# A new order of the routing stage in a fused attention and mixture-of-experts kernel

## The reference

```
xn   = layernorm(x)
out  = x + attention(xn) + shared(xn) + experts(xn)
attention: 16 heads of 128 in 4 groups that share k and v, causal softmax, dense 2048 -> 512
shared(xn) = relu(xn @ Ws1.T)**2 @ Ws2.T                 # 512 -> 512 -> 512
routing:   s = sigmoid(xn @ Wr.T + br)                   # 32 experts, 8 groups of 4
           keep the 4 groups with the largest sum of their two best; then the 6 best experts
           gate = 2.5 * s / sum of the six chosen s
experts:   sum over the chosen e of gate[e] * relu(xn @ W1[e].T)**2 @ W2[e].T
```

## Time and profile before

| | |
|---|---|
| median of 3 runs | 1601.65 us (1601.16 to 1601.92) |
| the profiled execution | 1600.37 us, of which the span of the instructions is 1598.6 us |
| PE busy in the span | 1551.1 us (97%) |
| DVE, ACT, POOL busy | 71%, 53%, 19% |
| chain that ended last | PE 94%, DVE 4%, ACT 1%, issue 1% |
| PE busy by 40th of the span (40 us each), tenths | 6897899899999999999999999999999999999998 |

### The profile page before, as it was taken

The page is one execution under the profiler, slowest core; times in us unless marked ns, Lnnn a source line. Parts: engine busy times, 40 slices in busy tenths (PEclk is TensorE's granted clock), DMA queues, the critical chain, the costliest instruction groups (busy, mean ns, idle before and its releaser), DMA issues.

```text
span 1598.6 us, 31303 instructions
## 1 busy us (share of the span) xinstructions
PE 1551.1 (97%) x8780; PEld 1331.9 (83%) x8781; DVE 1137.6 (71%) x2324; ACT 844.3 (53%) x1756; POOL 296.9 (19%) x542
## 2 busy tenths in 40 slices
PE   6897899999999999999999999999999999999998
PEld 5776789889889878888888888888888888888886
DVE  5586766665665638958967876876885895895886
ACT  3546466766666645535544544544553563553553
POOL 0000544444344401001011011011011111100101
PEclk9899899999999999999999999999999999999999
DMA  7492477777777631112011011422110211211101
GB/s 265 158 371 104 168 229 238 235 242 220 243 243 240 212 106 47 40 40 66 20 59 59 26 59 52 171 92 72 52 52 26 65 33 31 61 39 40 47 27 60
DMA packets 64758, 184.35 MB, mean 115 GB/s; under 512 B 7120, under 2 KB 7248, under 8 KB 59984
## 3 DMA queue, kind: packets, MB, share of 16 engines
q1 hardware_dynamic: 39872, 112.56, 20.1%
q0 software_dynamic: 16640, 54.54, 12.4%
q10 hardware_dynamic: 8208, 16.78, 2.7%
HBM read 123.29 MB, written 60.56 MB: 115 GB/s over the span
## 4 chain that ended last, share of the span: by engine, by line
PE 94%; DVE 4%; ACT 1%; issue 1%; DMA 0%; DVEq 0%; ACTq 0%; POOLq 0%
PE bank L650 9%; PE bank L652 9%; PE bank L651 9%; PE bank L955 8%; PE ps_s L650 6%; PE ps_s L652 6%; PE ps_s L651 6%; PE ps_s L943 5%; PE ps_s L944 4%; PE ps_s L938 4%; PE ps_s L821 4%; PE ps_s L844 3%; PE ps_s L825 3%; PE ps_s L822 3%; PE ps_s L845 3%; PE ps_s L848 3%
## 5 line engine op out<-in xcount | busy, mean ns | idle before, releaser
L1249 ACT ACTIVATE probs<-ps_s,negmax 128x128 f32<-128x128 f32 (+7 forms) x256 | 189.7, 741 | 173.9 <-DVE negmax L1624 172.3
L1276 DVE TENSOR_TENSOR pT_lo<-bank,pT_hi 128x512 fp32r<-128x512 f32 x288 | 196.4, 686 | 80.8 <-ACT pT_hi L1257 79.8
L1257 ACT ACTIVATE pT_hi<-bank 128x512 fp32r<-128x512 f32 x288 | 169.0, 596 | 142.9 <-PE bank L955 141.5
L1624 DVE TENSOR_REDUCE negmax<-ps_s 128x1 f32<-128x128 f32 (+7 forms) x256 | 189.4, 750 | 10.6 <-PE ps_s L944 8.0
L415 POOL TENSOR_TENSOR settled<-ident 128x1 f32<-128x1 f32 x192 | 55.4, 289 | 704.9 <-DVE acc L1651 695.2
L955 PE MATMUL bank<-ident,probs 128*128 128x128 f32 x1152 | 167.4, 272 | 1.1 <-DVE pT_lo L1276 1.1
L955 PEld LDWEIGHTS bank<-ident,probs 128*128 128x128 f32 x1152 | 139.6, 141 | 28.8 <-issue 1.3
L650 PE MATMUL ps_s<-xT_hi,wa_hi 128*128 128x512 f32 x384 | 153.5, 400 | 0.0
L652 PE MATMUL ps_s<-xT_hi,wa_lo 128*128 128x512 f32 x384 | 150.8, 393 | 0.0
L651 PE MATMUL ps_s<-xT_lo,wa_hi 128*128 128x512 f32 x384 | 149.9, 390 | 0.0
L943 PE MATMUL ps_s<-kT_lo,qT_hi 128*128 128x512 f32 (+3 forms) x384 | 142.4, 371 | 0.0
(11 more groups left out here) (198 smaller groups left out, 3700.1 us busy)
## 6 DMA issues: line engine op xcount, KB each, us to landing
eraw<-we SPq DMA_DIRECT2D x37, 1024.0 KB, 7.3
expert_outputs<-ysb SPq DMA_DIRECT2D x111, 256.0 KB
araw<-wa SPq DMA_DIRECT2D x37, 512.0 KB, 3.8
expert_outputs<-comb ACTq DMA_DIRECT2D x1, 16384.0 KB, 49.5
normed_tokens<-xn SPq DMA_DIRECT2D x4, 1024.0 KB, 6.9
out<-acc SPq DMA_DIRECT2D x16, 256.0 KB, 3.1
res<-x SPq DMA_DIRECT2D x2, 1024.0 KB, 6.7
acc<-x SPq DMA_DIRECT2D x2, 1024.0 KB, 13.9
```

The lines of the kernel that those rows point to most:

```text
L1249: act.activation(probs[:, i % 2, a, 0:keys], src, ACT.Exp, bias=negmax[:, i % 2, a:a + 1], accum_out=rowsum[:, i % 2, a:a + 1]).then_inc(e ...
L1257: act.activation(pT_hi[:, blk % RING, :], ps_t[blk % 2][:, :], ACT.Copy).then_inc(pt_hi_ready, 1)
L1276: dve.tensor_tensor(out_, whole, upper.bitcast(F32), ALU.subtract).then_inc(signal, 1)
L1624: dve.tensor_reduce(negmax[:, i % 2, a:a + 1], src, AX.X, ALU.max, negate=True).then_inc(max_ready, 1)
```

## The change

Nothing is computed otherwise. The change does five things.

1. The input comes in five parts instead of four halves (`PARTS`: two tiles, two tiles, four, then four and four of the other batch). The first tiles are normalized as soon as two of them are there, and the router's weights are loaded after four tiles instead of eight. The first four tiles of the other batch are normalized by DVE, only the last four by ACT.
2. PE begins with 16 products of 512 columns on a tile of ones (`warm(WARM)`), whose result nobody reads; POOL writes the ones first of all. Two more such products follow each of the first four logits.
3. The order of the stage on PE, ACT and DVE is written anew: the first two hidden products come ahead of tile 4, the logits of both batches are all done ahead of the first `outputs`, the routing of the first batch is earlier on DVE, and the list's products stand one or two at a time among the shared layers. The last three `outputs` follow the last list product in both kernels.
4. `find_gates` is cut into three steps for each batch (`match_rows`, `match_gates`, `sum_gates`), and these six steps are moved to DVE's part of the first attention group, one after each of K0, K1, P0, P1, Q00 and Q01.
5. DVE splits all four pieces of the first expert's weights right after the list, between the remaining `add_output`s; ACT too splits them ahead of the first gathered tile.

```diff
+PARTS = ((0, 0, 2), (0, 2, 4), (0, 4, 8), (1, 0, 4), (1, 4, 8))
+WARM = 16
...
-FIRST_ORDER = ("K0 K1 P0 P1 Q00 Q01 Q02 Q03 S00 E00 S01 E01 N00 X S02 E02 N01 S03 E03 N02 N03")
+FIRST_ORDER = ("K0 G0 K1 G1 P0 G2 P1 G3 Q00 G4 Q01 G5 Q02 Q03 S00 E00 S01 E01 N00 X S02 E02 N01 S03 E03 N02 N03")
...
-        ps_up = [[banks[0], banks[0]], [banks[0], banks[2]]]
+        ps_up = [banks[0], banks[2]]
...
+            def load_part(i):
+                s, lo, hi = PARTS[i]
+                sp.dma_start(residual[s][:, lo:hi, :], xb[:, batch_of(s) * NT + lo:batch_of(s) * NT + hi, :]).then_inc(x_in[i], 16)
+            load_part(0)
+            load_part(1)
...
+            load_part(2)
...
+            load_part(3)
+            load_part(4)
...
+            pool.memset(ones[:, :].bitcast(F32), 1.0).then_inc(ones_ready, 1)
...
+            def warm(n):
+                for _ in range(n):
+                    pe.matmul(ps_s[:, 0, :].rearrange("p (n c) -> p n c", n=CQ), ones[:, :],
+                              ones[:, :].unsqueeze(1).to_broadcast([P, CQ, P]), start=True, stop=True)
+            pe.wait_ge(ones_ready, 1)
+            warm(WARM)
+            pe.wait_ge(consts_ready, 9)
             pe.wait_ge(consts_in, 32)
...
-                if s or t >= 2:
-                    pe.wait_ge(xf_ready, n if s else n - 1)
-                bank = ps_up[1 - s][t % 2]
+                if n >= 2:
+                    pe.wait_ge(xf_ready, n - 1)
+                bank = ps_up[t % 2]
...
-                    pe.wait_ge(xf_ready, NT)
+                    pe.wait_ge(xf_ready, B * NT)
...
             turn_up(0, 0)
             turn_up(0, 1)
             logits(0, 0)
+            warm(2)
             turn_up(0, 2)
             logits(0, 1)
+            warm(2)
             turn_up(0, 3)
             logits(0, 2)
+            warm(2)
+            logits(0, 3)
+            warm(2)
+            hidden(0, 0)
+            hidden(0, 1)
             turn_up(0, 4)
-            logits(0, 3)
-            hidden(0, 0)
             turn_up(0, 5)
             logits(0, 4)
-            hidden(0, 1)
             turn_up(0, 6)
             logits(0, 5)
...
             logits(0, 7)
             hidden(1, 1)
             turn_up(1, 0)
-            hidden(2, 0)
             turn_up(1, 1)
             logits(1, 0)
+            hidden(2, 0)
             turn_up(1, 2)
             logits(1, 1)
-            hidden(2, 1)
             turn_up(1, 3)
             logits(1, 2)
+            hidden(2, 1)
             turn_up(1, 4)
             logits(1, 3)
-            outputs(0, 0)
+            hidden(3, 0)
             turn_up(1, 5)
             logits(1, 4)
             turn_up(1, 6)
             logits(1, 5)
-            outputs(0, 1)
+            hidden(3, 1)
             turn_up(1, 7)
             logits(1, 6)
+            logits(1, 7)
+            outputs(0, 0)
+            outputs(0, 1)
             outputs(0, 2)
-            logits(1, 7)
             outputs(0, 3)
-            for j in (3, 4):
-                for m in range(KM):
-                    hidden(j, m)
+            hidden(4, 0)
+            hidden(4, 1)
             ranks()
-            for q in range(CQ):
-                outputs(1, q)
+            outputs(1, 0)
+            outputs(1, 1)
+            outputs(1, 2)
+            outputs(1, 3)
             list_rows(0)
             hidden(5, 0)
             list_rows(1)
             hidden(5, 1)
             list_rows(2)
+            hidden(6, 0)
             list_rows(3)
-            hidden(6, 0)
+            hidden(6, 1)
             list_rows(4)
+            outputs(2, 0)
             list_rows(5)
-            hidden(6, 1)
+            outputs(2, 1)
             list_rows(6)
-            for q in range(CQ - 1):
-                outputs(2, q)
-                list_rows(2 * q + 7)
-                list_rows(2 * q + 8)
-            outputs(2, CQ - 1)
+            list_rows(7)
+            hidden(7, 0)
+            list_rows(8)
+            list_rows(9)
+            outputs(2, 2)
+            list_rows(10)
+            list_rows(11)
+            hidden(7, 1)
+            list_rows(12)
             list_rows(13)
-            hidden(7, 0)
+            outputs(2, 3)
             list_rows(14)
-            hidden(7, 1)
             list_rows(15)
-            for q in range(CQ - 1):
-                outputs(3, q)
+            outputs(3, 0)
+            outputs(3, 1)
+            outputs(3, 2)
...
+            def root(i):
+                s, lo, hi = PARTS[i]
+                act.wait_ge(std_ready, i + 1)
+                act.activation(std[:, s, lo:hi], rstd[:, s, lo:hi], ACT.Sqrt).then_inc(root_ready, 1)
...
+            def normalize_last():
+                act.wait_ge(shift_ready, 1)
+                act.wait_ge(xn_ready, NT + HALF)
+                act.wait_ge(xn_out[1], 16)
+                act.wait_ge(xnT_ready, NT)
+                for t in range(HALF, NT):
                     act.activation(xn[:, t, :], acc[:, t, :], ACT.Identity, bias=shift[:, t:t + 1],
                                    scale=rstd[:, 1, t:t + 1]).then_inc(xn_ready, 1)
...
                 upper_up(s, t)
-            root(0, 0)
-            root(0, 1)
-            both_up(0, 0)
-            both_up(0, 1)
+            root(0)
+            copy_up(0, 0)
+            upper_up(0, 0)
+            copy_up(0, 1)
+            upper_up(0, 1)
+            root(1)
             upper_shared(0, 0)
             upper_shared(0, 1)
-            both_up(0, 2)
-            both_up(0, 3)
+            copy_up(0, 2)
+            upper_up(0, 2)
+            copy_up(0, 3)
+            upper_up(0, 3)
             upper_shared(1, 0)
             upper_shared(1, 1)
-            both_up(0, 4)
-            root(1, 0)
-            both_up(0, 5)
+            root(2)
             relu_unit(0, 0)
-            root(1, 1)
-            both_up(0, 6)
             relu_unit(0, 1)
-            both_up(0, 7)
+            copy_up(0, 4)
+            upper_up(0, 4)
+            copy_up(0, 5)
+            upper_up(0, 5)
+            root(3)
+            copy_up(0, 6)
+            upper_up(0, 6)
+            copy_up(0, 7)
+            upper_up(0, 7)
             square_unit(0)
-            normalize(0)
...
+            def spread(i):
+                s, lo, hi = PARTS[i]
...
+            def shift_last():
+                s, lo, hi = PARTS[-1]
+                invert(len(PARTS) - 1)
+                dve.scalar_tensor_tensor(out=shift[:, lo:hi], in0=mv[:, s, lo:hi, 0], scalar=-1.0,
+                                         in1=rstd[:, s, lo:hi], op0=ALU.mult, op1=ALU.mult).then_inc(shift_ready, 1)
+            def normalize(i):
+                s, lo, hi = PARTS[i]
+                invert(i)
+                if s:
+                    dve.wait_ge(xn_out[0], 16)
+                    dve.wait_ge(xnT_ready, HALF)
+                for t in range(lo, hi):
                     dve.tensor_scalar(xn[:, t, :], residual[s][:, t, :], mv[:, s, t, 0:1], rstd[:, s, t:t + 1],
                                       ALU.subtract, ALU.mult).then_inc(xn_ready, 1)
...
+                dve.wait_ge(consts_ready, 9)
+                dve.wait_ge(xlo_ready, NT + 6)
...
-            spread(0, 0)
-            spread(0, 1)
-            normalize(0, 0)
-            normalize(0, 1)
+            spread(0)
+            normalize(0)
+            spread(1)
+            normalize(1)
+            lower_up(0, 0)
+            lower_up(0, 1)
             lower_shared(0, 0, 1)
             lower_shared(0, 1, 2)
-            for t in range(HALF):
-                lower_up(0, t)
-            spread(1, 0)
+            lower_up(0, 2)
+            lower_up(0, 3)
+            spread(2)
+            normalize(2)
             lower_shared(1, 0, 3)
             lower_shared(1, 1, 4)
-            spread(1, 1)
-            scale_and_shift(0)
+            spread(3)
             lower_up(0, 4)
+            normalize(3)
             lower_up(0, 5)
-            scale_and_shift(1)
+            spread(4)
+            take_logits(0)
             lower_up(0, 6)
             lower_up(0, 7)
-            take_logits(0)
+            shift_last()
             lower_unit(0)
-            for c in range(2, WP):
-                lower_shared(0, c, 3 + c)
+            lower_shared(0, 2, 5)
+            lower_shared(0, 3, 6)
             lower_up(1, 0)
+            route_groups(0)
+            lower_up(1, 1)
             lower_unit(1)
-            for c in range(2, WP):
-                lower_shared(1, c, 5 + c)
-            lower_up(1, 1)
```

173 lines of the change are left out of this document (83 added, 90 removed).

## The result

The changed kernel takes 1573.33 us (median of 4 runs, 1570.85 to 1576.05), the kernel before 1601.41 us beside it (4 runs, 1598.55 to 1601.92): a ratio of 0.983, 95% interval 0.9813 to 0.9848. The forecast was 1572.7 us. The profiled execution took 1576.05 us with a span of 1574.3 us; it was the slowest of the four.

A forecast was written before the change was run, and what follows sets the result against it. PE bounds the kernel, busy 97% of the span, not full only in the first 200 us. 20.5 to the list plus 8.5 behind it take 29.0 off 1600.37: 1571.4, median 1.3 above: 1572.7 us, range 1565 to 1583.

The forecast's parts named there:

- The start: First normalized tiles: PE starts real work at 10.05 us instead of 15.36, a gain of 5.3 us.
- The dummies take the level to 2.4 GHz and it holds from 10 us on: Front of PE: 16 dummies cost nothing, eight later ones 1.8 us; the stretch needs some 8 us less.
- Rival A: Clock level falls back during transposes, logits and pauses from 10 to 18 us; 5 to 7 us, about 1578.5; chance 0.2.
- The order up to the ranks: Shared layers before the ranks: 5.3 us lost instead of 19.4; ranks start at 76.0 us.
- Rival B: The new order saves no waits; only start, clock and the part behind the list remain: 1581.7 us; chance 0.1.
- the 19.4: Kernel before, up to the ranks: 78.2 us taken for 58.8 us of work, so 19.4 us counted as lost.
- The list: From the ranks' end: 46.8 us of products plus 8.1 lost; list at 136.2 us against 156.71, 20.5 us gained.
- From the list to the first output copy: Behind the list, ahead of the experts: 21 us instead of 29.5, so 8.5 us gained.
- the 1.63 us for `mhsq`: PE's wait behind the first expert tile: falls away with two others, together 6.6 us, as waits for DVE's gates.
- The gates in attention cost nothing: First attention group: DVE's idle time covers the six operations; cost 0, without cover 10.4 us.
- Rival C: The gates in attention are not covered: 10.4 us back, 1583 us; chance 0.04.
- Rivals D and E: D: front hidden anyway, 1594 us, chance 0.04; E: small waits hold PE at 1.2 GHz, about 1650, chance 0.01.

The follow-up runs named there:

- e11: e5 with the first batch's first four tiles as one part, 45 dummies ahead of the transposes and 3 behind the first logits: 1576.23 us.
- e12: The changed kernel with a second operation of the same size ahead of each of the six gate operations in attention: 1578.76 us.
- e9: The changed kernel with the edits of e5 and e8 together: 1564.29 us.
- e5: The changed kernel with 19 dummies instead of 16 at the start and 6, 3, 3 and 3 instead of 2 behind each logits: 1570.08 us.
- e7: The changed kernel run again, unaltered: 1574.23 us.
- e3: The changed kernel without any dummy products, neither the 16 at the start nor the 8 behind the logits: 1573.05 us.
- e4: The changed kernel with add_output(2, 3) moved on DVE from ahead of mark_rows(14) to behind lower_unit(7): 1572.94 us.
- e8: e4 with mark_rows(15) also moved ahead of square_unit(7) on ACT: 1568.64 us.
- e6: The kernel before with the gates moved to attention and all four first-expert weight pieces split ahead of the first gathered tile on DVE and ACT: 1592.86 us.
- e2: The changed kernel with the gates back between list and first tile and DVE's lower weight parts in the old order, ACT's order kept: 1580.95 us.
- e10: e9 with the second expert's four lower weight parts ahead of add_output(3, 3) on DVE: 1563.65 us.
- e1: The kernel before with the gates moved to attention and DVE's four lower first-expert weight parts earlier, ACT's order unchanged: 1596.16 us.

## Why the prediction came out right, step by step

- *The start*: 10.05 predicted, 9.26 measured. DVE began at 6.32 instead of the 7.1 that I scaled from the earlier trace rows. About half of the gain is DVE's order and not the smaller part, which I had not seen (e11).
- *The dummies take the level to 2.4 GHz and it holds from 10 us on*: the step that failed. The first half holds: 16 dummies in 5.3 us, so some of them at 0.23, though the level came within them and not after 6.9 us. That they cost nothing isn't always so: they took 6.6 us in e12 and 7.35 (19 of them) in e9, and PE started at 9.68 and 10.45. The second fails in both profiles of the changed kernel: the level fell near 13 us and stayed low until 26.6. Rival A, chance 0.2, describes it. Its price was right too: held (e5) and fallen (e7) differ by 5.6 us at the ranks and 4.1 us in the medians, against 5 to 7. With the level held, in e5 and e12, the ranks came at 75.91 and 76.17, against 76.0 predicted. Why it fell in five profiles of this front and held in one stays open.
- *The order up to the ranks*: right in size, as these two show. The wait at the fourth `outputs` was put at 1.8 and measured 0.90. That the level and not the order was off is what e3 adds: without dummies and with the level low until about 25 us the ranks come at 80.45, still 13 us earlier than before, of which the start gives 4.5. Rival B is out. My reading of the losses was incomplete, though. The 15.4 us of waiting in the earlier trace rows lie ahead of the first product and aren't part of the 19.4. In those are 6.0 us of waits (62.10 less 56.15), the 8 of the clock, and some 4 that I left out: around this wait of the kernel before the granted clock was 0.50, from about 52 to 62 us (the 0.92 of the earlier trace rows).

```profile
54.28 1.08 PE L669 MATMUL bank<-ident,xn 128*128 128x128 f32 x4 [3.30 <-ACT xf L1032]
```

  The changed kernel waits 1.5 us in all there, and the level doesn't fall again.
- *The ranks* took 4.09 us instead of 5.30, 1.2 that I hadn't counted; the earlier trace rows have a granted clock of 0.77 there, the changed kernel 1.00, and this pause ahead of them in the kernel before is gone:

```profile
93.58 1.96 PE L720 MATMUL bank<-rsel,ones 128*128 128x32 f32 x16 [1.17 <-DVE rcross L1388]
```

- *The list*: 53.33 us against 54.9. The 3.5 us wait for `add_output(2, 3)` is there (4 predicted), but e4 and e8 show that it was only half the cause: ACT's `row_hot` was as late.
- *From the list to the first output copy*: 21.3 against 21; gain 8.2 against 8.5. e6 and e2 give 8.4 and 8.3 in their traces, 7.0 and 6.7 to 7.6 in the medians. The first expert tile starts at 152.55, 13.6 behind the list rather than 12.5, and no wait for `wa_lo` is left. That `eraw` arrives in time is seen too. But one term failed: the 1.63 us for `mhsq`, which I laid to the gates, is still there with 1.67. It hangs on DVE's lower parts of the second expert's weights, as e10 shows, where it falls to 0.50. So the sum of this stretch is right although one of its terms was not.
- *The gates in attention cost nothing*: no wait of PE for `kT_lo` or `qT_lo` is new. Rival C is out, but e12 shows little room. Attention is 1.6 us longer all the same. The windows of before and after from 19 us behind K0's lower part on (596.81 and 570.84):

```profile
596.81:606.81 10.00, 7.48 (x50) 6.70 (x51) 7.82 (x22) 5.38 (x17) 0.51 (x1) 1.00 0.01 2
```

```profile
570.84:580.84 10.00, 8.61 (x42) 8.13 (x43) 6.71 (x21) 4.99 (x17) 1.91 (x2) 0.66 0.30 80
```

  The granted clock is 0.66 instead of 1.00: the level fell behind the pause of 1.41 us that both kernels have, and the first combination comes 29.0 instead of 27.7 us behind K0. In e2, which has no gates there, it is 0.86 and attention takes 1022.9 us, so this isn't the gates' doing by itself. Of the 13 profiles with this pause of 1.41 us, only the kernel before's reads 1.00 there; the twelve others read 0.60 to 0.86 and take 1021.8 to 1024.1 us for attention, so its 1020.8 may be the lucky case. What decides it stays open.

The sum against the profiled execution, 1576.05 - 1571.4 = 4.65 us: 5.6 for the level, less 1.2 for the ranks and 1.6 for the list, 0.3 behind the list, 1.6 in attention, together 4.7. The medians hide this: the profiled execution is the slowest of its set, and runs at 1570.2 and 1570.9 lie where a held level would put it (1576.05 - 5.6 = 1570.4). My last term, the median 1.3 us above the profiled execution, had the wrong sign too: here it lies 2.7 below, 4.0 us that take back most of the 4.65. So that 1572.7 is 0.6 us from the median is luck: most likely the median mixes both outcomes of rival A, and not every term was right. Rivals D and E are out: the experts began 25.95 us earlier and took as long as before. (Two of the rivals' times were added up wrongly: D's is 1601.65 - 8.5 = 1593, and E's, with 107 us more than the forecast, about 1680 and not 1650.)

## What to carry to other kernels

Where a wait is removed, ask who is queued behind it on every engine: twice here, in e1 and e4, the second engine had the same delay in its own queue, and only the pair of moves paid. Dummy products paid here when 34 of them filled the pause to its end and led up to the first dense work; 24 that left it open bought nothing at the median, and a wider spread (5.9 us against 2.3 without any). A profiled execution shows one outcome of such a chance, so its milestones and the medians should be reconciled term by term.
